# A hybrid attention / FFN / state-space block on one core: set-up merged with the first batch, zero matmuls taken out, and a new table of steps

## What is computed

```
x = x + attention(layernorm(x))     # 16 heads of 16, latent width 32, rope, causal softmax
x = x + ffn(layernorm(x))           # fp4_linear(silu(fp4_linear(x, gate)) * fp4_linear(x, up), down)
x = x + mamba(layernorm(x))         # two directions, 512 channels x 16 states, scan over the tokens
x = x + ffn(layernorm(x))           # the same weights
def fp4_linear(x, w): quantise x and w in blocks of 16 to the grid 0, .5, 1, 1.5, 2, 3, 4, 6 times a scale, then x @ w.T
```

## Time and profile before

| | |
|---|---|
| median of 3 executions | 4221.96 us (4219.04 to 4224.25) |
| the profiled execution, its own time | 4215.24 us |
| its span, first to last instruction | 4213.5 us |
| mean granted TensorE clock | 0.948 |
| set-up (start to the first statistics of batch 0's `x`) | 137.7 us |
| batch 0 alone, until the first scan | 137.7 to 427.6 us |
| each batch of units, batches 1 to 6 | 488.5 to 490.2 us |

### The profile page before, as it was taken

How to read it: one execution, slowest core, us unless ns; L and a number is a source line. 1 busy time by engine, 2 the same in 40 slices (tenths; PEclk the granted TensorE clock), 3 DMA queues, 4 the chain that set the end, 5 groups by cost and what they waited for, 6 DMA issues and landing times.

```text
span 4213.5 us, 41483 instructions
## 1 busy us (share of the span) xinstructions
PE 3521.7 (84%) x13488; PEld 1871.2 (44%) x13488; DVE 3054.1 (72%) x4294; ACT 2036.8 (48%) x3852; POOL 1927.2 (46%) x1154
## 2 busy tenths in 40 slices
PE   5886798789988898879988899888988899879657
PEld 5553354245543454435543455434544355434214
DVE  3243768877687867877788776878678777887993
ACT  0354464635645455534655346544555346463441
POOL 0100744546444454445545464544544454453760
PEclk9997899999999999999999999999999999999998
DMA  3002544744446444364436444464454645364780
GB/s 84 1 1 79 190 148 130 248 166 159 142 139 237 143 142 165 137 231 138 152 133 214 157 162 147 143 233 137 136 167 147 220 143 156 128 219 145 268 275 5
DMA packets 203816, 649.64 MB, mean 154 GB/s; under 512 B 34253, under 2 KB 45520, under 8 KB 197456
## 3 DMA queue, kind: packets, MB, share of 16 engines
q1 hardware_dynamic: 203600, 646.98, 45.8%
HBM read 595.52 MB, written 51.38 MB: 154 GB/s over the span
## 4 chain that ended last, share of the span: by engine, by line
PE 48%; DVE 17%; issue 17%; ACT 11%; POOL 6%; SPq 1%; DMA 1%; POOLq 0%; DVEq 0%; ACTq 0%
PE banks L1268 18%; PE banks L1512 9%; DVE banks L844 7%; PE banks L1449 6%; PE banks L1297 5%; PE banks L1273 5%; ACT banks L1234 4%; DVE sb_arena L851 4%; PE banks L1425 3%; POOL sb_arena L980 3%; DVE sb_arena L772 2%; ACT sb_arena L1017 2%; SPq L427 1%; POOL sb_arena L892 1%; ACT sb_arena L1020 1%
## 5 line engine op out<-in xcount | busy, mean ns | idle before, releaser
L980 POOL TENSOR_TENSOR sb_arena<-sb_arena 128x1024 f32<-128x1024 f32 x512 | 1210.2, 2365 | 807.6 <-PE banks L1512 543.6
L844 DVE TENSOR_TENSOR_SCAN banks<-banks,sb_arena 128x512 f32<-128x512 f32 x1024 | 1197.9, 1215 | 212.3 <-ACT banks L1234 163.2
L1512 PE MATMUL banks<-sb_arena,sb_ident 128*128 128x512 f32 x2048 | 1041.0, 636 | 335.4 <-DVE sb_arena L851 266.0
L1234 ACT ACTIVATE banks<-sb_arena,sb_neg_a 128x512 f32<-128x512 f32 x1024 | 665.3, 682 | 1062.1 <-DVE sb_arena L851 1053.5
L1512 PEld LDWEIGHTS banks<-sb_arena,sb_ident 128*128 128x128 f32 x2048 | 386.6, 201 | 824.4 <-DVE sb_arena L851 434.1
L1017 ACT ACTIVATE sb_arena<-banks 128x512 f32<-128x512 f32 (+4 forms) x752 | 381.1, 519 | 582.8 <-PE banks L1273 389.1
L851 DVE TENSOR_TENSOR sb_arena<-banks,sb_arena 128x512 f32<-128x512 f32 x1024 | 650.5, 676 | 0.0
L1273 PE MATMUL banks<-sb_ident,sb_arena 128*128 128x128 f32 (+1 forms) x2082 | 343.8, 287 | 219.3 <-ACT sb_arena L1017 85.6
L1273 PEld LDWEIGHTS banks<-sb_ident,sb_arena 128*128 128x128 f32 (+1 forms) x2082 | 244.2, 145 | 429.7 <-ACT sb_arena L1017 156.7
L723 DVE TENSOR_REDUCE sb_nmax<-banks 128x1 f32<-128x512 f32 (+3 forms) x352 | 222.9, 636 | 290.9 <-PE banks L1452 289.4
L1449 PE MATMUL banks<-sb_arena 128*128 128x384 f32 (+3 forms) x1024 | 358.7, 461 | 0.7 <-issue 0.7
(11 more groups left out here) (126 smaller groups left out, 4027.3 us busy)
## 6 DMA issues: line engine op xcount, KB each, us to landing
sb_arena<-rows_bc SPq DMA_DIRECT2D x1024, 512.0 KB, 4.5
kept_xc<-sb_arena SPq DMA_DIRECT2D x16, 1024.0 KB, 5.0
kept_z<-sb_arena SPq DMA_DIRECT2D x16, 1024.0 KB, 4.4
sb_arena<-kept_z SPq DMA_DIRECT2D x64, 256.0 KB, 5.0
sb_arena<-kept_xc SPq DMA_DIRECT2D x64, 256.0 KB, 4.9
kept_zs<-sb_arena SPq DMA_DIRECT2D x8, 1024.0 KB, 6.6
sb_arena<-kept_zs SPq DMA_DIRECT2D x8, 1024.0 KB, 9.7
sb_xin<-in_x SPq DMA_DIRECT2D x8, 512.0 KB, 7.6
```

Source lines behind the costliest of these rows:

```text
L844: v.tensor_tensor_scan(factors, factors, products, 0.0, ALU.mult, ALU.add).then_inc(V.sem, V.mark("scan", K, e))
L980: nc.gpsimd.tensor_tensor(dBu[K % SLOTS], u[:, p % 2].unsqueeze(1).to_broadcast([P, 2, T]), rows_b[K % BS], ALU.mult).then_inc(G.sem, G.ma ...
L1234: nc.scalar.activation(psum[:, e], dt[:, (K // NQ) % 2], ACT.Exp, scale=neg_a[:, s, m, 2 * q + e:2 * q + e + 1]).then_inc(A.sem, A.mark("d ...
L1512: mm = pe.matmul(psum[:, YB], ident[:, :], dBu[K % SLOTS][:, e], start=(q == 0 and e == 0), stop=(q == NQ - 1 and e == 1))
```

## The change

It has three parts.

1. **Set-up.** The loads are in three groups with a semaphore each: 19 that the fold needs (`s_fold`, issued without waiting for the memsets), then `x` of batch 0, then 18 with the rope tables, the FFN weights and the attention's other weights (`s_mid`), then 19 (`s_w`). The fold spreads the small projection into a block-diagonal matrix (`bd`, `bdv`, for the 8 heads that 128 channels hold) and needs 8 matmuls of 128x512 for `w_lat`, and 4 of 128x128 for `w_v`. The quantisation of the FFN weights is done in between the visits of batch 0's latents, one chunk per four visits, and the turning of them after batch 0's attention.
2. **PE.** `keep_busy`, `zerob` and `summing` are gone.
3. **Table.** `VISITS` has other numbers in all seven rows. The slots are those of before but for `ffn1`, 11 for 12, and `early`, 13 for 12.

```diff
 # sync
+            for dst, src in fold_loads:
+                sp.dma_start(dst, src, allow_slow_non_contiguous=True).then_inc(s_fold, 16)
+            sp.dma_start(xin[:, :, :], x_dram[0]).then_inc(s_xin, 16)
             sp.wait_ge(V.sem, V.at("cleared"))
+            for dst, src in mid_loads:
+                sp.dma_start(dst, src, allow_slow_non_contiguous=True).then_inc(s_mid, 16)
             for dst, src in loads:
                 sp.dma_start(dst, src, allow_slow_non_contiguous=True).then_inc(s_w, 16)
 # vector
+            front = beside(None, 0)
+            advance(front, MERGE_N + 1)
+            v.wait_ge(s_mid, MID)
+            v.wait_ge(A.sem, A.at("w_v"))
             for i in range(3 * CK):
...
                 grid(qn_w[i % 2], qm_w[i % 2], "w", i)
-            v.wait_ge(A.sem, A.at("set_up"))
-            v.wait_ge(E.sem, E.at("set_up"))
-
-            drain(beside(None, 0))
+                advance(front, 4)
+            advance(front, LAT_N + ATT_N - 1 - 4 * 3 * CK)
+            v.wait_ge(s_w, LOADED)
...
+            drain(front)
 # tensor
-            def keep_busy():
-
-                if summing[0]:
-                    pe.matmul(psum[:, YB], zerob[:, :], identb[:, :].unsqueeze(1).to_broadcast([P, T // P, P]),
-                              start=False, stop=False)
...
             def ffn(b, f):
                 for i in range(FFN_N):
-                    keep_busy()
...
             def prep(n):
                 for i in range(PREP_N):
-                    keep_busy()
...
-            pe.wait_ge(s_w, LOADED)
+            pe.wait_ge(s_fold, FOLD)
             accumulate(psum[0:17, 0, 0:HD], [(kv2l_a, l2oT), (e16[:, :], lob)], "mt17")
+            pe.wait_ge(V.sem, V.at("rep16"))
+            for w in range(2):
+                accumulate(psum[:, 1 + 6 * w, 0:2 * L], [(rep16, qk17[0:HD, w])], "rep", w)
             pe.wait_ge(V.sem, V.at("mt17"))
+            accumulate(psum[:, 2, 0:HD], [(rep16, mt17[0:HD])], "rep_v")
             for w in range(2):
+                pe.wait_ge(V.sem, V.at("bd", w) if w == 0 else V.at("bdv"))
+                for h in range(2):
                     for k in range(CK):
+                        accumulate(psum[:, fold_bank(w, h, k)],
+                                   [(wat[:, CK * w + h, k * P:k * P + P], bd[w].rearrange("p h l -> p (h l)"))],
+                                   "w_lat", w, h, k)
...
+            pe.wait_ge(A.sem, A.at("w_v"))
+            pe.wait_ge(s_mid, MID)
+
+            front = beside(None, 0)
+            advance(front, MERGE_N + LAT_N + ATT_N)
             pe.wait_ge(G.sem, G.at("wq", 2 * CK - 1))
```

More of the change, by code:

```diff
@@ L26 @@
 H, HD, L = 16, 16, 32
+HPC = P // HD
 HL = H * L
@@ L150 @@
 VISITS = {
[L151 to L158, removed]
+    "merge": (1, 1, 2, 3, 4, 0, 0, 2, 2, 3),
+    "ffn2": (0, 1, 5, 7, 7, 1, 8, 2, 3, 3, 7, 1, 5, 3),
+    "lat": (4, 0, 1, 2, 2, 0, 3, 2, 0, 7, 1, 1, 1, 0, 2),
+    "att": (0, 0, 4, 0, 2, 0, 3, 1, 0, 5, 1, 1, 0, 1, 1, 6, 0, 1, 0, 3, 1, 2,
+            0, 5, 0, 2, 0, 4, 1, 1, 0, 1, 0, 3, 1, 3, 2, 0, 2, 0, 3, 0, 3, 0, 2),
+    "ffn1": (4, 2, 14, 3, 2, 13, 8, 0, 4, 0, 3),
+    "early": (5, 0, 1, 0, 2, 0, 0, 2, 10, 2, 1, 0, 2),
+    "late": (0, 0, 2, 0, 0, 0, 0, 0, 0, 1, 0, 2, 2, 0, 0),
 }
@@ L443, in merge @@
                                 sp.wait_ge(s_rows[s], done)
[L444 to L446 removed]
+                        if n is not None and n >= 1:
+                            sp.wait_ge(V.sem, V.at("attended", n - 1, TT - 1))
                             sp.dma_start(xin[:, :, :], x_dram[n]).then_inc(s_xin, 16)
@@ L1541, in _ @@
             for h in range(H):
-                accumulate(psum[0:1, 3, h * HD:h * HD + HD], [(bq17[:, 2 * H + h:2 * H + h + 1], mt17)],
-                           *(("w_v",) if h == H - 1 else ()))
-            pe.wait_ge(G.sem, G.at("wq", 2 * CK - 1))
-            pe.wait_ge(A.sem, A.at("w_v"))
-            for i in range(2 * F // P):
-                for k in range(CK):
-                    last = i == 2 * F // P - 1 and k == CK - 1
-                    turn(psum[:, 3 * k + i // 4, (i % 4) * P:(i % 4) * P + P],
-                         rows_gu[:, i * C + k * P:i * C + k * P + P], *(("w_gu",) if last else ()))
+                accumulate(psum[0:1, 6, h * HD:h * HD + HD], [(bq17[:, 2 * H + h:2 * H + h + 1], mt17)],
+                           *(("b_v",) if h == H - 1 else ()))
@@ new lines, in _ @@
+            pe.wait_ge(A.sem, A.at("w_v"))
+            pe.wait_ge(s_mid, MID)
+            front = beside(None, 0)
+            advance(front, MERGE_N + LAT_N + ATT_N)
+            pe.wait_ge(G.sem, G.at("wq", 2 * CK - 1))
+            for k in range(CK):
+                for i in range(2 * F // P):
+                    c = i // 4
+                    if k >= 1 and i % 4 == 0:
+                        pe.wait_ge(A.sem, A.at("w_gu", k - 1, c))
+                    turn(psum[:, c, (i % 4) * P:(i % 4) * P + P], rows_gu[:, i * C + k * P:i * C + k * P + P],
+                         *(("w_gu", k, c) if i % 4 == 3 or i == 2 * F // P - 1 else ()))
@@ L1559, in _ @@
             pe.wait_ge(A.sem, A.at("set_up"))
-            accumulate(psum[0:17, 7, 0:1], [(e16[:, :], ones[0:1, 0:1])], "set_up")
-            drain(beside(None, 0))
+            pe.wait_ge(s_w, LOADED)
+            drain(front)
             for b in range(B):
```

150 lines of the change are left out of this document (86 added, 64 removed).

## The result

| | before | after |
|---|---|---|
| median of 4 executions beside each other | 4220.5 us (4218.95 to 4224.25) | 3981.74 us (3978.26 to 3986.93) |
| ratio | | 0.9434, 95% interval 0.9418 to 0.945 |
| span of the profiled execution | 4213.5 us | 3985.1 us |
| mean granted TensorE clock | 0.948 | 0.937 |

The account below looks back on a forecast made before the run. It took PE to bound `merge`, and PE and DVE, both nearly full, to alternate in the FFN stages. 4215.2 - 90 (set-up) - 92 (zeros) + 28 (clock), table 0, gave 4061; plus 6.8 for the median, 4068 us, range 3990 to 4140.

Parts of the forecast that it names:

- The set-up: Start of the kernel, before the first scan: -108 + 12 + 6 = -90 us, bounds -109 and -47.
- the first turn: PE's first turn of batch 0's normalised `x`: starts near 36 us instead of 143.7, 108 us earlier.
- Given back: Set-up work moved later: 12 us for quantisation chunks in the latents, 6 for turning the FFN weights behind the attention.
- The zeros: 872 zero matmuls in FFN and prep, 187 us of PE: removal gains 92 us, less 28 for the clock.
- what of it is on the path: Zero matmuls per batch: at most a unit's length less DVE's busy time counts, 13.2 us a batch, x 7 = -92.
- five units: Five listed units: removing zeros gains 2.8, 1.5, 1.8, 2.4 and 1.7 us, together 10.2 a batch.
- The other 71 zeros: Units where DVE is as good as full: 15.3 us of PE a batch, a fifth counted, 3 us.
- The 4 us a batch for the clock: FFN and prep stages: lower clock grants without zeros cost 4 us a batch, +28, ends 0 and +176.
- the third rival: FFN and prep: grants fall as in batch 0 alone, half on the path, +88 against -92: 4128 us, chance 0.21.
- The table at 0, -40 to +40: New `VISITS` numbers in all seven stages: costed at 0 us, with -40 to +40.
- the slack: Room over the busier engine: 0, 11.3, 10.7, 5.1 and 7.4 us a batch; 6 won or lost, times 7, is 42.
- The second rival: FFN stages go down to DVE's busy time through the table, 145 us instead of 64: 3987 us, chance 0.15.

Follow-up runs that it names:

- no_zeros: The kernel before without its two calls of `keep_busy` (in ffn and prep), nothing else changed: 4203.28 us, ratio 0.9963.
- zeros_back: The changed kernel with `keep_busy`, `zerob` and `summing` put back in ffn and prep: 4009.84 us, ratio 0.9503.

## Why the prediction was wrong

**The set-up was right in place and near in size.** -100 to -102 measured, -90 forecast. By its terms: the first turn stands at 27.0 and not at 36. The 19 issues for the fold took 0.41 us each (0.7 to 8.4 us) where the prediction used 0.78, and the fold began at 9.7 for 15; from there it took 13.8 us for 20.7. The 18 issues of `s_mid` did take 0.79 each, and that load, landed by 27.0 for 30, came last, not the fold. (The trace has 56 loads before, not 55, which changes no term.) Given back were 14.7 us for 18: the latents are 50.0 us for 43.0 (+7, forecast +12), and turning, FFN and prep together +6.4 (forecast +6), attention +1.3.

**The zeros were oversized by far.** The step that failed is "what of it is on the path", 13.2 us a batch: a unit's length less DVE's busy time was taken as room in which each zero counts. `no_zeros` shows at most 5.9 us a batch in its place. Of the 10.2 us from five units, the first and the fourth gave 4.5 of 5.2; the third and the fifth gave 0.1 of 3.5, though PE was busy for nearly all of them, and the chain that held the fifth has no zero in it; the second, with 1.5, lost 2.2 by the clock. The other 71 zeros, good for 3 us by the prediction, gave at most 1.3. PE's idle time in these stages, 13.1 us of 72.5 in `ffn2`, already said that others held a part of their units. The 4 us a batch for the clock were right in size (4.2 in three units), leaving out the two units that grew for an unknown reason, and they are on the path in a unit in which PE pauses and in `early`. The net, 9.2 us a batch in the forecast, was 2.4 by the medians.

**The rule of the third rival.** The grants fell without zeros (0.91 and 0.95 to 0.86 and 0.90 in the FFNs of `no_zeros`), and that took back most of what their units gained. The rival's own numbers were too large on both sides, and the time fell by 16.6 us all the same. The Trainium skill, page "TensorE: Matmul & The Clock Gate", section "HAM oscillation — how this bites in real kernels", which the prediction cited, says that waits of PE bring the slow clock back and advises a loop order in which PE stays warm. The grants agree with the first; filling PE's gaps with zeros did not pay here, narrow, single or double.

**The table at 0, -40 to +40, is the error that took the time out of the range.** It gave -107 alone. Two things failed. The slack was summed over `merge`, the FFNs and prep; the attention, the longest stage, with PE idle for 14 of 158 us, was not in it. And the slack was taken over DVE's busy time as if that were fixed; 44 us of it went with a new order of the work, most of them contention with POOL. The second rival (3987) had the right time by luck: it expected the FFN stages to drop by 20.7 us a batch, and they dropped by 4.2.

**Sum.** -100 set-up, -107 table, -17 zeros make -224. The whole is -239. Of the 15 between, 11 are the zeros again, which cost 28 and not 17 beside the new table; 4 are left, with `zeros_back` (set-up and table together) at -210 where the two alone make -207. Luck kept the miss small: the table gave 107 us more than forecast and the set-up 10, but the zeros 36 less (28 for 64), so the errors partly cancel.

## What to carry to other kernels

Before a table of steps is costed at nothing, list the slack of every stage over its busiest engine, the longest stage first, and look whether the busy time itself is stretched: the same instruction at several durations is the sign. In a stage where engines hand small results to each other, work in front of an engine's own wait and work behind it are not the same, even with the same instructions. An engine that is busy for nearly all of a unit need not hold it: look for the filler on the critical chain before pricing its removal. And a stage whose length stays the same can hide two effects that cancel, here shorter work against a slower clock; the lengths of its units show them.

## What the runs showed of the hardware

DVE and POOL stretch each other. A 128x32 `TENSOR_SCALAR` of 0.18 us took 1.90 beside a POOL product that reads SBUF. A convolution (two inputs in SBUF) takes 0.68 to 0.74 us alone and 1.11 (18.89/17) beside a stream of 128x256 POOL products, which themselves take 1.11 then (16.63/15) and 0.72 at the least: both lose. A unit's two scans, which read one input from PSUM and one from SBUF, did not: their median is 2.34 us in the kernel before, both in the 268 units where POOL works beside them for most of that time and in the 83 where it does not work at all.

Twelve matmuls of 128x256 in f32 took 3.07 us at the grant of 1.00 and 5.27 in a unit with 0.67, in which PE had idled before them.
